# A vision tower on one core: expert shares spread by DMA instead of by matmul, and a new order of work in the last stage

## The chip, the cores and the metric

One core of a Trainium2 chip runs the whole program in one launch. The metric is device time in microseconds (us), median of the runs. TensorE (PE) multiplies matrices, VectorE (DVE), ScalarE (ACT) and GpSimd (POOL) do elementwise work, SyncE (SP) issues most DMAs. Each engine works through its own list of instructions in order; semaphores tie the lists together.

## The reference, cut to what matters

Four images of 3136 patches plus two class tokens go through a token embedding, a state-space layer, an expert layer that picks 1024 tokens per expert, then windowed attention and a second expert layer. The change touches this last part:

```python
# windowed attention: windows of 64 tokens, 8 heads of 16
out = softmax(q k * SCALE) v ;  h = h + (out @ w_proj.T + b_proj)
# second expert layer, on n = layernorm(h)
h_shared = swiglu(n @ shared_in_w.T);  out_shared = h_shared @ shared_out_w.T
# a group of 4 experts per token, softmax over its 4, the best 2 kept, shares normalised
comb[token, expert], cnt[token, expert]            # share, and 0/1 for "chosen"
h_expert = swiglu(n @ expert_in_w.T)
routed = cnt @ expert_out_bias + sum_e comb[:, e] * (h_expert @ expert_out_weight[e].T)
```

All eight experts share `h_expert`, so expert e costs one scaling of `h_expert` by its share (VectorE) and one product with its weights (TensorE), summed in one PSUM bank.

## The kernel before, in words

The program has three stages, one after the other on every engine: phase A (state-space layer), phase B (first expert layer), phase C (`phase_c`, attention and second expert layer). Phase C works on 12,800 token rows as 25 groups of 512 columns (`NG`, `GW`). It is a software pipeline of turns: in one turn `L` is the group whose rows are loaded and normalised, `A` the group in attention, `N` the group whose heads are projected and normalised again, `U` the group whose hidden rows are made (eight products `up0` to `up7`) and whose gates are read, `X` the group that goes through the experts. Four turns fill the pipeline, four drain it. Inside a turn, every engine's list is an order written out by hand at the end of its function; `BANK_ORDER` must tell the same order of use for each of the eight PSUM banks.

What the steps of the prediction touch:

- `turn_o` (L1653) transposes the attention result on TensorE, `keep_o` (L1790) copies it to SBUF as `ot`, SP writes it to DRAM (`heads`, L1586), waits, and reads it back in another order with eight DMAs (`dealt`, L1589). `project` (L1691, L1695) multiplies `dealt` by the projection weights and adds the residual `x` by four products with the identity. SP's list holds, ahead of L1586, the store of the previous group's result (L1567), which waits for `finish` on VectorE (L1900).
- `choose_experts` writes shares, in three copies on partitions 32, 64 and 96 of `cc`, and the 0/1 rows. `turn_choice` (L1638) transposes them. ScalarE and VectorE split the shares into three bf16 parts that add up to the fp32 value (L1777, L1939, L1783, L1944). For each expert `spread` (L1672) multiplies by a selection matrix, so that row e stands on all 128 partitions of a PSUM bank (`CB0`, `CB1`). `scale` (L1957) multiplies the two hidden tiles by it, into a ring of three (`sc`), and `expert` (L1680) multiplies by the expert's weights.
- On ScalarE, after `center` and `variance`: `square`, `norm_rows` (L1834) for group L, `column_scale` (L1841, L1843), `silu_table` (L1797), `affine` (L1848); at the start of the next turn `silu(0)`, `keep_n3` (L1769).
- POOL makes attention's products: scores (L2089) from each `qkv_copy`, and values (L2096) once VectorE's `probs` (L1983) is done.
- Before phase C's first turn SP waits for phase B's last scatter, then issues 13 loads of weights (L1573, L1574), then the first rows (L1579).

An fp32 product appears as two MATMUL records in the trace, a bf16 product and a transpose as one.

Of the kernel before, what the change touches and what calls it, by code (L numbers as in the profile page):

```python
# [17 lines left out]
P = 128  # L18
# [67 lines left out]
def build(nc, a, out, upto="C", debug=None):  # L86

    debug = debug or {}
    with ExitStack() as ctx:
# [893 lines left out]
def phase_b(nc, ctx, mem, a, h_rows, n_rows, logits, after_a, progs):  # L983
# [103 lines left out]
    def sync(sp):  # L1087
# [16 lines left out]
    def vector(dve):  # L1104
# [49 lines left out]
        for r in range(DIGITS):  # L1154
# [218 lines left out]
    def gpsimd(pool):  # L1373
        after_a(pool)
        pool.memset(ones[:], 1.0).then_inc(s_fill, 1)
# [24 lines left out]
        for e in range(E0):  # L1400
            if e + XG - 1 < E0:
# [46 lines left out]
def phase_c(nc, ctx, mem, a, h_rows, out, after_b, progs):  # L1448
# [10 lines left out]
    SC_RING = 3  # L1459
    ident, cen_w, mean_w = sb("ident", [P, P]), sb("cen_w", [P, P]), sb("mean_w", [P, P])  # L1460
    w_qkv = sb("w_qkv", [P, 3 * D])
    w_proj = sb("w_proj", [P, D])
    w_up = sb("w_up", [P, 4 * HF])
    w_so = sb("w_so", [P, 2, D])
    w_ex = sb("w_ex", [P, 2, E1 * D])
    w_gate = sb("w_gate", [P, NGATE])
    gate_b = sb("gate_b", [P, NGATE])
    bias9 = sb("bias9", [E1 + 1, D])
    cols = sb("cols", [P, 3])
    eps_cols = sb("eps_cols", [P, 2])  # L1470
    picks = sb("picks", [P, E1])
# [702 lines left out]
```

## Time and profile before

| | |
|---|---|
| median of 3 runs | 2853.29 us (2849.75 to 2855.03) |
| the profiled execution | 2854.72 us, its span 2852.9 us |
| phase C in it | from the first load at 1819.89 us to the end |
| busy share of the span | PE 85%, DVE 82%, POOL 68%, ACT 54% |
| mean granted TensorE clock | 0.934 of full speed |

Shares over the span average three stages with different limits, so they don't say what bounds phase C; the windows of that phase do. A group's busy time counts overlapping records once.

### The profile page before, as it was taken

The page shows a single profiled execution, that of the slowest core. Times are in us where ns is not written, and L with a number is a line of the kernel's source. Part 1 is how long each engine was busy: PE and PEld are TensorE (multiplying, and loading weights), DVE is VectorE, ACT ScalarE, POOL GpSimd, SP SyncE. Part 2 cuts the span into 40 slices and gives each one's busy share as a digit, 9 for nine tenths or more (in the row PEclk, how much of TensorE's full clock was granted, in tenths as well). Part 3 has the DMA queues.
Part 4 walks back from the last instruction along what each step waited for, and adds up shares of the span by engine and source line. Part 5 has one row for each costly group of instructions (what it writes and reads, how often), then busy time and mean ns, then how long its engine had stood idle before and what let it go on. Part 6 is the DMA issues. An engine that isn't in the chain of part 4 may idle for free. (4 is left out here: it accounts for less than half of the span.)

```text
span 2852.9 us, 25309 instructions
## 1 busy us (share of the span) xinstructions
PE 2417.9 (85%) x6774; PEld 1128.9 (40%) x6774; DVE 2351.7 (82%) x3447; ACT 1544.7 (54%) x2598; POOL 1946.2 (68%) x1008
## 2 busy tenths in 40 slices
PE   5999999999999999999861397159999999899988
PEld 2444444444444444444321143024444444444443
DVE  2999999999999999999978522158887888888875
ACT  4777777777776777777632153134344444344332
POOL 2898898988989889898950388565555555555540
PEclk8999999999999999999975598559999999999999
DMA  2333433334333333433320043300101000011000
GB/s 75 101 120 92 124 105 113 108 95 123 103 112 106 104 118 100 124 98 110 114 82 0 20 70 56 57 22 26 30 30 30 26 28 24 26 30 30 26 23 11
DMA packets 169759, 199.28 MB, mean 70 GB/s; under 512 B 38969, under 2 KB 156946, under 8 KB 169490
## 3 DMA queue, kind: packets, MB, share of 16 engines
q1 hardware_dynamic: 158354, 189.27, 21.6%
q0 software_dynamic: 11264, 8.40, 2.2%
q8 instruction: 56, 0.92, 0.1%
q14 instruction: 85, 0.70, 0.1%
HBM read 164.37 MB, written 33.25 MB: 69 GB/s over the span
## 5 line engine op out<-in xcount | busy, mean ns | idle before, releaser
L915 POOL TENSOR_TENSOR a_hc<-a_h,a_cs 128x896 f32<-128x896 f32 (+1 forms) x448 | 859.5, 1938 | 55.8 <-DVE a_h L778 55.6
L362 PE MATMUL a_y_bank<-a_hc,a_ident 128*128 128x448 f32 (+1 forms) x1792 | 741.8, 544 | 21.8 <-DVE a_yz L798 21.2
L553 ACT ACTIVATE a_da<-a_dt,a_neg_a 128x448 f32<-128x448 f32 (+1 forms) x896 | 551.9, 631 | 296.0 <-DVE a_h L778 291.0
L778 DVE TENSOR_TENSOR_SCAN a_h<-a_da,a_h,a_dbx 128x448 f32<-128x448 f32 x528 | 582.9, 1133 | 9.5 <-ACT a_da L553 4.4
L2096 POOL TENSOR_TENSOR c_prod<-c_prob,c_qkv 128x1024 f32<-128x1024 f32 x100 | 280.8, 2848 | 272.2 <-DVE c_prob L1983 272.2
L362 PEld LDWEIGHTS a_y_bank<-a_hc,a_ident 128*128 128x128 f32 x1792 | 331.5, 190 | 326.3 <-issue 272.6
L1680 PE MATMUL c_p_ACC<-c_sc,c_w_ex 128*128 128x512 f32 x800 | 363.7, 592 | 0.0
L762 DVE TENSOR_TENSOR a_dbx<-a_dtx,a_b_bank 128x896 f32<-128x896 f32 (+1 forms) x308 | 327.3, 1063 | 16.2 <-PE a_b_bank L355 16.1
L2089 POOL TENSOR_TENSOR c_prod<-c_qkv 128x1024 f32<-128x1024 f32 x100 | 231.8, 2341 | 153.2 <-ACT c_qkv L1764 153.2
L1957 DVE TENSOR_TENSOR c_sc<-c_hid,c_p_CB 128x1024 f32<-128x1024 f32 x200 | 240.0, 1214 | 68.5 <-PE c_p_CB L1672 65.8
L903 POOL TENSOR_TENSOR a_dbp<-a_dtx,a_bs 128x896 f32<-128x896 f32 (+1 forms) x140 | 270.9, 1935 | 0.0
L778 DVE TENSOR_TENSOR_SCAN a_h<-a_da,a_h,a_dbp 128x448 f32<-128x448 f32 x240 | 263.1, 1128 | 0.0
L1680 PEld LDWEIGHTS c_p_ACC<-c_sc,c_w_ex 128*128 128x128 f32 x800 | 151.7, 190 | 182.0 <-issue 179.4
L1613 PE MATMUL c_p_W<-c_fl,c_w_up 128*128 128x512 f32 x400 | 211.3, 624 | 9.5 <-ACT c_fl L1848 8.2
L1758 ACT ACTIVATE c_act_half<-c_p_W 128x512 f32<-128x512 f32 x100 | 59.9, 599 | 251.0 <-PE c_p_W L1613 248.9
L405 PE MATMUL a_work<-a_xn,a_w_tap 128*128 128x448 f32 (+1 forms) x448 | 187.3, 552 | 3.7 <-ACT a_xn L694 3.7
L355 PE MATMUL a_b_bank<-a_bc,a_sel 128*128 128x448 bf16 (+1 forms) x308 | 110.2, 358 | 73.5 <-DVE a_dbx L762 71.5
L1385 POOL DMA_INDIRECT b_xg<-n_rows,b_index x64 | 62.3, 974 | 141.2 <-DVE b_tab L1255 122.0
L1991 DVE TENSOR_REDUCE c_o<-c_prod 128x128 f32<-128x1024 f32 x100 | 117.2, 1211 | 38.7 <-POOL c_prod L2096 38.7
L1964 DVE TENSOR_REDUCE c_score<-c_prod 128x64 f32<-128x1024 f32 x100 | 121.2, 1212 | 20.2 <-POOL c_prod L2089 18.0
L932 POOL TENSOR_TENSOR a_spl<-a_spl,a_yt 128x896 f32<-128x896 f32 (+1 forms) x28 | 58.6, 2094 | 90.3 <-DVE a_yt L805 68.0
L1764 ACT COPY c_qkv<-c_p_T 128x384 f32<-128x384 f32 x100 | 49.0, 490 | 130.7 <-PE c_p_T L1645 123.1
(304 smaller groups left out, 3718.2 us busy)
## 6 DMA issues: line engine op xcount, KB each, us to landing
a_cs<-c_rows SPq DMA_DIRECT2D x96, 896.0 KB, 5.2
a_bs<-c_rows SPq DMA_DIRECT2D x24, 1120.0 KB, 5.6
a_cs<-c_rows SPq DMA_DIRECT2D x16, 900.0 KB, 4.4
c_x<-h_rows SPq DMA_DIRECT2D x25, 256.0 KB, 2.7
heads<-c_ot SPq DMA_DIRECT2D x25, 256.0 KB, 2.3
c_dealt<-heads SPq DMA_DIRECT2D x200, 32.0 KB, 1.9
rolled<-c_res SPq DMA_DIRECT2D x25, 256.0 KB, 2.1
h_rows<-a_th SPq DMA_DIRECT2D x24, 224.0 KB
```

Of the source, the lines that this page charges most:

```text
L362: pe.matmul(y_bank[:, d, 0:g.w], ident[:], hc[:, (g.i * NS + n) % HC_RING, d, 0:g.w], start=(n == 0), stop=(n == NS - 1)).then_inc(s_sum, 1)
L405: mm = pe.matmul(tile_of(use, p)[:, 0:w], w_tap[:, j, d * P:(d + 1) * P], xn[:, j:j + w], start=(j == 0), stop=(j == KC - 1))
L553: act.activation(da[:, k % DA_RING, 0:g.w], dt[g.slot][:, d, 0:g.w], ACT.Exp, scale=neg_a[:, d * NS + n:d * NS + n + 1]).then_inc(s_da, 1)
L762: dve.tensor_tensor(dbx[:, k % DBX_RING, :, 0:g.w], dtx[g.slot][:, :, 0:g.w], b_bank[:, 0:g.w].unsqueeze(1).to_broadcast([P, 2, g.w]), ALU ...
L778: dve.tensor_tensor_scan(h[:, n, d, 0:g.w], da[:, (g.i * 2 * NS + k) % DA_RING, 0:g.w], x, state, ALU.mult, ALU.add).then_inc(s_scan, 1)
L903: pool.tensor_tensor(dbp[:, k % DBP_RING, :, 0:g.w], dtx[g.slot][:, :, 0:g.w], bs[:, POOL_STATES.index(n), 0:g.w].unsqueeze(1).to_broadcas ...
L915: pool.tensor_tensor(hc[:, (q.i * NS + n) % HC_RING, :, 0:q.w], h[:, n, :, 0:q.w], cs[:, n % C_RING, 0:q.w].unsqueeze(1).to_broadcast([P, ...
L1613: end(f"up{m}", U, pe.matmul(p[:], w_up[:, m * P:(m + 1) * P], fl[U % 2][:], start=True, stop=True))
L1680: mm = pe.matmul(p[:], w_ex[:, i, e * D:(e + 1) * D], sc[:, k % SC_RING, i, :], start=False, stop=(e == E1 - 1 and i == 1))
L1957: dve.tensor_tensor(sc[:, k % SC_RING, :, :], hid[X % 2][:, 2:4, :], tile_of(f"cb{e}", X)[:].unsqueeze(1).to_broadcast([P, 2, GW]), ALU.mu ...
L2089: pool.tensor_tensor(prod[j][:].rearrange("p (h g d) -> p h g d", h=NH, g=NH), q.rearrange("p (h d) -> p h d", d=DH).unsqueeze(2).to_broad ...
L2096: pool.tensor_tensor(prod[j][:].rearrange("p (h d g) -> p h d g", h=NH, g=NH), prob[:, j * NH:(j + 1) * NH, :].unsqueeze(2).to_broadcast([ ...
```

## The change

- **Shares.** The 0/1 rows now stand three times (partitions 0, 32, 64) and the shares once, on partitions 96 to 103. ScalarE's `keep_choice` copies the shares to `c_s` (fp32) and the 0/1 rows to `c_b` (bf16). SP writes `c_s` to DRAM (`share_out`, 16 KB). ScalarE then waits for that DMA in `share_in` and issues, from its own queue, two DMAs of 1 MB that read four share rows each and write them to all 128 partitions (`c_all`, ring of four halves). The eight `spread` products, the bf16 splitting, `sel_e`, `picks` and the two `CB` banks go.
- **Hidden rows.** The two expert tiles of `hid` are written to the two freed banks (`hx`, in PSUM). `scale(e)` multiplies `hx` by the share row in SBUF.
- **Biases.** One bf16 product of the 0/1 rows with three bf16 parts of the biases, in place of one fp32 product.
- **Projection.** The residual goes first, by four transposes into the projection's bank, and the product with `dealt` is added after its wait. The bank is now `T`, not `M`.
- **Order.** `BANK_ORDER` and all lists of a turn are new. SP stores the previous result after it has issued `heads`. On ScalarE `column_scale` comes ahead of `norm_rows`, and `silu_table` last, behind `affine`.
- **Loads.** Phase C's weights are loaded in phase B (SP's list, at its third expert); their tiles are allocated ahead of phase B's. POOL's first memsets in phase B wait for an early VectorE count.

```diff
-BANK_ORDER = (("up0", "W0", "U"), ("up1", "W1", "U"), ("n3", "T", "A"), ("up2", "W0", "U"), ("up3", "W1", "U"),
...
+BANK_ORDER = (("n3", "T", "A"), ("up0", "W0", "U"), ("qkv0", "M", "A"), ("qkv1", "T", "A"), ("up1", "W1", "U"),
+              ("up2", "W0", "U"), ("trans", "M", "X"), ("gates", "R", "U"), ("o", "M", "N"), ("qkv2", "T", "A"),
+              ("up3", "W1", "U"), ("qkv3", "M", "A"), ("up4", "W0", "U"), ("acc", "ACC", "X"), ("up5", "W1", "U"),
+              ("up6", "W0", "U"), ("proj", "T", "N"), ("cen", "M", "N"), ("up7", "W1", "U"), ("var", "T", "N"))
...
 # SP, one turn
+            load()
+            share_out()
+            heads_out()
+            store_last()
+            heads_in()
...
 # ScalarE
+            def share_in():
+                if X is not None:
+                    act.wait_ge(s_rows[X % 2], (X // 2 + 1) * 16)
+                    for half in range(2):
+                        if X >= 2:
+                            for e in range(half * EG, half * EG + EG):
+                                scaled(act, X - 2, e)
+                        r = X % 2 * 2 + half
+                        act.dma_start(c_all[:, r, :, :], share_rows[X % 2][half * EG:(half + 1) * EG, :].partition_broadcast(P)
+                                     ).then_inc(s_all[r], 16)
...
 # VectorE
+                    dve.tensor_tensor(sc[:, n % SC_RING, :, :], hx[:], shares(dve, X, e), ALU.mult
+                                      ).then_inc(s_sc, 1)
...
 # TensorE
+                    for j in range(GT):
+                        pe.matmul(p[:, j * P:(j + 1) * P], x[N % 3][:, j, :], ident[:], is_transpose=True,
+                                  start=(j == 0), stop=False, skip_group_check=True)
                     pe.wait_ge(s_dealt[N % 2], (N // 2 + 1) * (16 * 8))
+                    mm = pe.matmul(p[:].rearrange("c (w h a) -> c w h a", h=NH, a=8), w_proj[:],
+                                   dealt[N % 2][:].rearrange("p h (w a) -> p w h a", a=8), start=False, stop=True,
+                                   skip_group_check=True)
```

The new lists of a turn, TensorE: `turn_n3, up(0), qkv_mm(0), qkv_mm(1), up(1), up(2), turn_choice, gates, turn_o, qkv_mm(2), up(3), qkv_mm(3), up(4), shared, up(5), up(6), biases, project, expert(0) to expert(5), center, up(7), variance, expert(6), expert(7)`. ScalarE: `keep_n3, silu(0), qkv_copy(0), keep_choice, qkv_copy(1), keep_o, qkv_copy(2), silu(1), share_in, qkv_copy(3), silu(2), silu(3), exp_table, gate_exp, row_scale, score_exp, keep_h3, square, column_scale, norm_rows, affine, silu_table`. VectorE: `choose_experts, sum_values(N, 2), sum_values(N, 3), hidden(0), finish_last, stats_of, sum_scores(0), choose_group, hidden(1), sum_scores(1), sum_scores(2), scale(0) to scale(2), sum_scores(3), scale(3), less_top, scale(4), scale(5), probs, scale(6), scale(7), hidden(2), less_mean, sum_values(A, 0), hidden(3), rescale, sum_values(A, 1)`.

## Rows read from the trace of the kernel before

**Rows 1.** Busy time of each engine in one turn, and in 21 turns.

```profile
core 0: us, PE busy (x) PEld busy (x) DVE busy (x) ACT busy (x) POOL busy (x), PEclk, DMA share, GB/s
2501.78:2538.51 36.73, 34.46 (x105) 16.32 (x104) 31.91 (x68) 15.40 (x29) 20.56 (x9) 1.00 0.10 29
1969.89:2763.84 793.95, 737.54 (x2175) 352.05 (x2174) 668.88 (x1418) 320.05 (x580) 428.31 (x167) 0.98 0.09 28
```

**Rows 2.** Timeline of one turn: start, duration, engine, line.

```profile
2498.13 0.60 PE L1653 MATMUL c_p_M<-c_ident,c_o 128*128 128x128 f32 x4
...
2499.19 1.06 ACT L1790 COPY c_ot<-c_p_M 128x512 f32<-128x512 f32 x1
...
2501.78 0.36 SPq L1567 DMA_DIRECT2D rolled<-c_res  x1
...
2502.18 0.43 SPq L1586 DMA_DIRECT2D heads<-c_ot  x1
...
2504.50 3.63 SPq L1589 DMA_DIRECT2D c_dealt<-heads  x8
...
2509.71 1.10 PE L1691 MATMUL c_p_M<-c_dealt,c_w_proj 128*128 128x512 f32 x2 [2.02 <-DMA c_dealt<-heads]
...
2534.86 0.60 PE L1653 MATMUL c_p_M<-c_ident,c_o 128*128 128x128 f32 x4
```

**Rows 3.** Groups of instructions in the 21 turns.

```profile
L1957 DVE TENSOR_TENSOR c_sc<-c_hid,c_p_CB 128x1024 f32<-128x1024 f32 x168 | 202.1, 1214 | 48.7 <-PE c_p_CB L1672 46.0
...
L1691 PE MATMUL c_p_M<-c_dealt,c_w_proj 128*128 128x512 f32 x42 | 30.0, 806 | 49.1 <-DMA c_dealt<-heads 49.1
...
L1939 DVE TENSOR_TENSOR c_p_M<-c_p_M,c_c_b 40x512 f32<-40x512 f32 x21 | 14.9, 709 | 14.4 <-ACT c_c_t L1778 14.4
```

**Rows 4.** The chain that ended last: start, duration, what.

```profile
2510.80 0.89 PE c_p_M L1695 x8
...
2812.99 1.72 PE c_p_ACC L1680 x4
2814.93 1.72 PE c_p_ACC L1680 x4
```

**Rows 5.** Windows of 2 us behind a wait for `dealt`.

```profile
2052.00:2054.00 2.00, 2.00 (x8) 1.48 (x7) 1.35 (x2) 0.00 (x0) 0.00 (x0) 0.50 0.00 0
```

**Rows 6.** Timeline at the start of phase C.

```profile
1819.89 0.33 SPq L1573 DMA_DIRECT2D c_ident<-in_ident  x1
...
1826.97 1.53 SPq L1579 DMA_DIRECT2D c_x<-h_rows  x3
...
1832.59 0.87 DVE L1912 BATCH_NORM_STATS2 c_stats<-c_x 128x6 f32<-128x128 f32 x4
```

**Rows 7.** DMA issues: KB each, median us from issue to landing.

```profile
a_cs<-c_rows SPq DMA_DIRECT2D x96, 896.0 KB, 5.2
a_bs<-c_rows SPq DMA_DIRECT2D x24, 1120.0 KB, 5.6
...
c_rows<-a_bcr SPq DMA_DIRECT2D x24, 84.0 KB, 5.2
```

**Rows 8.** Timeline of the last turn.

```profile
2828.53 0.19 DVE L2047 TENSOR_TENSOR c_cc<-c_share,c_p_R 128x48 f32<-128x48 f32 x1
...
2833.22 3.48 DVE L1957 TENSOR_TENSOR c_sc<-c_hid,c_p_CB 128x1024 f32<-128x1024 f32 x3 [0.56 <-PE c_p_CB L1672]
```

**Rows 9.** Timeline of ScalarE at the end of a turn.

```profile
2522.99 1.65 ACT L1834 ACTIVATE c_n<-c_x,c_shift,c_rstd 128x128 f32<-128x128 f32 x4 [3.38 <-DVE c_shift L1925]
...
2524.54 0.67 ACT L1841 ACTIVATE c_lv<-c_p_T,c_eps_cols 128x512 f32<-128x512 f32 x1
...
2525.96 1.28 ACT L1797 ACT_TABLE_LOAD   x1
...
2527.26 0.81 ACT L1848 ACTIVATE c_fl<-c_u,c_cols 128x512 f32<-128x512 f32 x1
...
2532.38 0.59 ACT L1769 COPY c_nt<-c_p_T 128x512 f32<-128x512 f32 x1 [0.70 <-PE c_p_T L1620]
```

More of the change, by code:

```diff
@@ L1445, in bank_table @@
     return nth
-def phase_c(nc, ctx, mem, a, h_rows, out, after_b, progs):
+SHARE, PARTS = 96, (0, 32, 64)
+KB = PARTS[-1] + E1 + 1
+@dataclass
+class Fixed:
+    ident: object
+    cen_w: object
+    mean_w: object
+    w_qkv: object
+    w_proj: object
+    w_up: object
+    w_so: object
+    w_ex: object
+    w_gate: object
+    gate_b: object
+    cols: object
+    eps_cols: object
+    earlier: object
+    later: object
+    bias9: object
+    bias_b: object
+    cc: object
+    s_in: object
+    s_const: object
+    loads: int
@@ L1496, in phase_c @@
     act_half = [sb(f"act_half{i}", [P, GW]) for i in range(2)]
-    hid = [sb(f"hid{s}", [P, 4, GW]) for s in range(2)]
-    cc = sb("cc", [P, GT, P])
-    c_t = sb("c_t", [E1 + 1, GW])
+    hid = [sb(f"hid{s}", [P, 2, GW]) for s in range(2)]
     c_b = sb("c_b", [P, GW], BF16)
+    c_s = sb("c_s", [P, GW])
+    c_all = sb("c_all", [P, ALL_RING, EG, GW])
     sc = sb("sc", [P, SC_RING, 2, GW])
@@ L1542, in phase_c @@
     s_sq, s_lv, s_r12, s_fl = map(sem, ("sq", "lv", "r12", "fl"))
-    s_route, s_gexp, s_c_b, s_c_r, s_c_m, s_comb, s_ex = map(
-        sem, ("route", "gexp", "c_b", "c_r", "c_m", "comb", "ex"))
-    LOADS = 13
+    s_route, s_gexp, s_c_s, s_comb, s_ex, s_sc = map(
+        sem, ("route", "gexp", "c_s", "comb", "ex", "sc"))
+    s_rows = [sem(f"rows{s}") for s in range(2)]
+    s_all = [sem(f"all{r}") for r in range(ALL_RING)]
     R_DIF, R_END = 8, 24
@@ new lines, in sync, with load, store, store_last @@
+        for X, U, N, A, L in turns:
+            def load():
+                if L is not None:
+                    if L >= 3:
+                        result(sp, "proj", L - 3)
+                    sp.dma_start(x[L % 3][:], h_rows[L * GW + SHIFT:(L + 1) * GW + SHIFT, :].rearrange(
+                        "(j p) d -> p j d", p=P)).then_inc(s_x[L % 3], 16)
+            def store(c):
+                if c is not None and c >= 0:
+                    taken(sp, "acc", c)
+                    sp.dma_start(out[:, c * GW:(c + 1) * GW], res[c % 2][:]).then_inc(s_res[c % 2], 16)
+            def store_last():
+                if X:
+                    store(X - 1)
+            def heads_out():
+                if N is not None:
+                    taken(sp, "o", N)
+                    sp.dma_start(heads[N % 2], ot[:]).then_inc(s_heads[N % 2], 16)
+            def heads_in():
+                if N is not None:
+                    s = N % 2
+                    sp.wait_ge(s_heads[s], (N // 2 + 1) * 16)
+                    for j in range(8):
+                        sp.dma_start(dealt[s][j * DH:(j + 1) * DH, :, :],
+                                     heads[s][:, j, :].rearrange("(h d) c -> d h c", d=DH)).then_inc(s_dealt[s], 16)
+            def share_out():
+                if X is not None:
+                    sp.wait_ge(s_c_s, X + 1)
+                    sp.dma_start(share_rows[X % 2], c_s[SHARE:SHARE + E1, :]).then_inc(s_rows[X % 2], 16)
+            load()
[3 more added lines that the diff above has]
+            heads_in()
@@ L2065, in vector @@
             scale(2)
-            stats_of()
             sum_scores(3)
```

331 lines of the change are left out of this document (162 added, 169 removed), and 5 rows, old and new, of the table BANK_ORDER.

## The prediction

> **What bounds the kernel now.** I read phase C alone, since phases A and B keep their work. The windows come first [rows 1]: in a turn of 36.73 us TensorE is busy for 34.46, VectorE for 31.91, POOL for 20.56. No engine fills the turn, so something goes round in it. The timeline [rows 2] shows what. Follow one heads trip: `turn_o` ends at 2498.73, the copy `ot` at 2500.25, SP issues `heads` only at 2502.18, it has landed when the eight `dealt` DMAs begin at 2504.50, and `project` starts at 2509.71, after TensorE stood idle for 2.02. That is 10.98 us. From there TensorE works without a gap worth naming to the end of the next `turn_o` at 2535.46, 25.75 us. The two make 36.73: this loop is the turn. The mean of 21 turns is 793.95 / 21 = 37.81 [rows 1], 1.08 more. [...]
>
> So an instruction off TensorE's list counts only if it lies in the 25.75, and time off the heads trip counts in full.
>
> **The first part of the loop, 10.98 us.** In SP's new list the store (L1567) no longer stands ahead of `heads`. From the end of `ot` to the issue passed 2.18 less 0.25, 1.93 us, while SP waited for `finish` and issued the store [rows 2]; only some 0.05 of it stays, but I leave that out. `share_out` now stands ahead of `heads`; its data are ready before `turn_o` starts, and its issue of 0.4 us (as L1567) is over by then. So 9.05 us.
>
> New here is traffic. `share_in` issues 2 MB some 2.4 us behind `turn_o`, just as `heads` is on its way and before `dealt` is issued. The nearest rows [rows 7]: 896 KB land in 5.2 us and 1120 KB in 5.6, so I take 5.4 for the first megabyte, and the second about 3 us later. All eight `dealt` DMAs then share the engines with it. How much later `dealt` lands no row shows. Lower bound 0. Upper bound: `dealt` is served behind both megabytes, which land at about 2.4 + 0.4 + 8.4 = 11.2 us after `turn_o`, plus a little, against 9.05: 2.5 us. The nearest row for a small DMA in such company is `c_rows`, 84 KB in 5.2 us [rows 7], where `heads` with 256 KB and no company takes 2.32 [rows 2]; but it is behind big ones in the same queue. [...]
>
> [...]
>
> **The second part, 25.75 us.**
> - Six of the eight spreads lie in it. One costs what it adds between two experts: 2814.93 - 2812.99 - 1.72 = 0.22 [rows 4]. 6 x 0.22 = 1.32 off. (VectorE's idle waits for a spread, 48.7 us in 21 turns [rows 3], lie beside TensorE's work and give nothing more.)
> - The residual's eight records, 0.89 [rows 4], go ahead of the wait, where TensorE idles: 0.89 off.
> - `up(6)` moves ahead of the wait and `up(3)` behind `turn_o`. Two products (four records) take 1.72 [rows 4], one 0.86: 1.72 off.
> - `qkv_mm(1)` (384 columns of 512: 0.65), `turn_choice` (four transposes, about 0.44) and `gates` (eight small records, 0.89 as the residual's eight) move into it: 1.98 on.
> - `turn_o` now follows `turn_choice` in bank M and must wait for both copies of `keep_choice`, 0.6 us each (as L1769 [rows 9]) and hand-overs, 1.3 against `gates` 0.89: 0.4 on.
> - A new wait: `qkv_mm(0)` now comes second, after `up(0)`, and needs `keep_n3`. On ScalarE it stands behind a row of work that starts when `variance` ends: hand-over 0.2, the two passes of `column_scale` 1.4 (2524.54 to 2525.96), `norm_rows` 1.65, `affine` 0.81, the table 1.28, `keep_n3` 0.59 [rows 9], together 5.9. Before, the table load stood in the wait for `affine`'s input and cost nothing; `affine` now waits behind `norm_rows`, so that cover is gone. TensorE meanwhile has experts 6 and 7 (3.44), four transposes 0.44, `up(0)` 0.86: 4.75. Queued behind it: `qkv_copy(0)`, and POOL's score products. 1.15 on.
>
> Sum: 25.75 - 1.32 - 0.89 - 1.72 + 1.98 + 0.4 + 1.15 = 25.35. Adding up forward what the new list holds from `project` to `turn_o` gives 24.8 (no small friction in it; the same for the old list gives 25.2 against 25.75). I take 25.05, and keep 24.8 and 25.35 as ends.
>
> **The loop.** 9.05 + 25.05 = 34.1. With 0.6 for traffic 34.7, and 1.1 for clock and stray long turns as before (the idle wait ahead of `project` is much the same: 9.65 less the 7.1 us of work behind `turn_o` and a stall or two) 35.8. Against 37.81: 2.0 a turn.
>
> **Other loops that could be longer.** VectorE: 31.91 less two splitting passes of 0.71 [rows 3] is 30.5. `scale` keeps one operand in PSUM and one in SBUF, so I leave 1.21 us; were it 10% dearer, 1 us a turn, still under 34.1. TensorE: 34.46 less 8 x 0.22 less 0.4 for the residual less 0.9 for the biases, 31.4. POOL: the value products start when `probs` is done, `qkv_copy(0)` waits for them, then come the score products, together 20.56 [rows 1], then on VectorE a reduction of 1.2 and what leads to `probs`; with copies about 26 us. All under 34.1. The old first wait in VectorE's turn, for POOL, is covered by `choose_experts`, which now comes first.
>
> **The shares' trip.** `turn_choice` ends; `c_s` 0.6; DMA to DRAM about 2.2 (nearest: 2.32 for `heads` [rows 2]); ScalarE reaches `share_in` 4.2 us after `turn_choice` because of the copies ahead of it, so the landed rows aren't waited for; then 5.4. `scale(0)` can start 9.6 us after `turn_choice`, `expert(0)` at 10.9. `project` begins 0.9 + 0.4 + 0.44 + 9.05 = 10.8 after it and ends 0.86 later. So 0.8 us is spare: hidden, barely. Uncovered, each further us costs one per turn.
>
> **The ends.** Start: 13 loads stood ahead of the rows; L1579 moves from 1826.97 to 1819.89 and `stats_of` no longer waits for the last weight. With the 2.32 that 256 KB of `heads` take [rows 2] it starts at 1822.3 against 1832.59 [rows 6]: 10 off. If the load took the 5.2 of `c_rows` [rows 7], it would be 7. The loads in phase B run beside a stage whose wait is not for SP; POOL's wait there is for an early VectorE count, long before its lists are used: 0. Filling: the turn of X = 0 gains a full turn's 2. Drain: in the last turn nothing covers the shares' trip. Shares to `scale(0)` took 4.5 us [rows 8]; now 0.8 + 0.6 + 2.2 + 5.4 = 9, and `expert(0)` waits for the first scaling too: 4.3 later, with 1.8 of spreads back. With the turn before: 2 on.
>
> **Sum.** 22 x 2.0 = 44, 10, 2, less 2: 54 off the profiled execution's 2854.72, 2801; the median of the runs is 1.4 lower, so **2799 us**.
>
> **The rivals.**
> - **The wait for `dealt` shrinks and the clock stays up.** The traffic costs nothing, the idle wait is 1 us, the clock never falls: 33.85 to 34.1 a turn, 3.8 x 22 = 84 and 10: 2759, down to 2750. For it: the store was 1.93 of the trip. Against: 2 MB a turn. 0.25.
> - **The traffic eats the gain.** `dealt` lands behind the megabytes: 2.5 on, and the longer idle lets the clock fall every turn, 1.6 on (a half-clock stretch of some 3 us, of which [rows 5] shows two, costs half its length): 38.2, or 37.4 if it falls in half of them. 22 x 0.4 either way, and 10: 2834 to 2852, its middle 2843. [...] 0.18.
> - **The shares come late (slower).** Place: `scale(0)` behind `c_all`. If a megabyte from ScalarE's queue takes over 10 us in place of 5.4, the 0.8 spare is gone, the turn is over 38.3 with the clock's share, and the start's 10 us are used up. At 11 us: 22 x 1.2 less 10: 2870. Against: 1120 KB landed in 5.6 [rows 7]. 0.09.
> - **Nothing moves** (the loop is another than I think, all edits beside it): only the start, 2843. 0.03.
>
> The forecast has 0.45, its own range 2780 to 2818 (traffic 0.2 to 1.4, second part 24.8 to 25.35). The whole range, 2755 to 2845, leaves out the late shares, half of the first rival's lower end and part of the second's upper. A measurement of this kernel tells 0.2% (6 us) from no change. Faster: 0.45 + 0.25 + most of 0.21 = 0.86; same 0.05; slower 0.09.
>
> **What would show it.** Heads trip near 9.6 us, `heads` issued within 0.1 of `ot`; `project`'s idle wait of 1.5 to 2.5; a gap of about 1 us before `qkv_mm(0)` put down to `keep_n3`; `dealt` landing later behind its last issue than before; `c_all` at 5 to 6; `stats_of` at 1823; DVE busy near 30.5 a turn. It is wrong if `scale` waits for `c_all` in each turn, if `dealt` lands 2 us later, or if VectorE rather than the heads trip closes the turn.

## The result, and the profile after

The changed kernel takes 2907.18 us (median of 4 runs, 2905.07 to 2910.9), against 2852.88 beside it: a ratio of 1.0185, interval 1.0167 to 1.0203. It is slower by 54 us, where the forecast was faster by 54.

The windows, with the columns of [rows 1]: one turn, then 20 turns.

```profile
2566.79:2607.70 40.91, 33.67 (x93) 15.68 (x92) 32.67 (x67) 14.94 (x28) 20.52 (x9) 0.92 0.24 78
1993.04:2811.64 818.60, 667.28 (x1810) 310.81 (x1809) 649.78 (x1307) 295.47 (x531) 405.99 (x159) 0.92 0.23 77
```

A turn is 818.60 / 20 = 40.93 us, against 37.81 before and 35.8 in the forecast. TensorE is busy for less time than before [rows 1], though at half clock for part of it, and waits more. The timeline of one turn, as [rows 2], shows where:

```profile
2564.00 0.28 SPq L1688 DMA_DIRECT2D share_rows<-c_c_s  x1
...
2565.33 1.06 ACT L1885 COPY c_ot<-c_p_M 128x512 f32<-128x512 f32 x1 [0.37 <-PE c_p_M L1756]
...
2566.14 0.33 ACTq L1877 DMA_DIRECT2D c_c_all<-share_rows  x1
2566.41 0.34 SPq L1675 DMA_DIRECT2D heads<-c_ot  x1
...
2566.63 0.71 ACTq L1877 DMA_DIRECT2D c_c_all<-share_rows  x1
2566.79 0.56 SPq L1666 DMA_DIRECT2D rolled<-c_res  x1
...
2572.22 3.48 DVE L2034 TENSOR_TENSOR c_sc<-c_hx,c_c_all 128x1024 f32<-128x1024 f32 x3
...
2573.18 4.02 SPq L1682 DMA_DIRECT2D c_dealt<-heads  x8
...
2578.63 2.08 PE L1790 MATMUL c_p_T<-c_dealt,c_w_proj 128*128 128x512 f32 x2 [5.89 <-DMA c_dealt<-heads]
...
2600.58 0.88 PE L1748 MATMUL c_p_M<-c_w_qkv,c_nt 128*128 128x384 f32 x2 [0.86 <-ACT c_nt L1857]
```

`heads` is issued 0.02 us behind the copy `ot`: the store is out of its way, as forecast. But `dealt` begins only 6.77 us later, where 2.32 had passed before [rows 2]. `project` starts 13.34 us behind `turn_o` (its end, 2565.29, is 0.04 ahead of the copy), where 9.05 was expected without traffic. The first megabyte was issued 0.27 us *ahead* of `heads`. ScalarE's DMA issue doesn't stand behind its copy in progress: L1877 is issued at 2566.14, 0.25 us before the copy ends at 2566.39, and `silu(1)`, ahead of it in the list, only starts at 2566.59.

The page's list of DMA issues (KB each, median us to landing), as [rows 7], shows that every transfer that starts there is slow; `dealt`, issued when the megabytes are nearly through, isn't:

```profile
c_c_all<-share_rows ACTq DMA_DIRECT2D x50, 1024.0 KB, 7.5
...
heads<-c_ot SPq DMA_DIRECT2D x25, 256.0 KB, 7.3
c_dealt<-heads SPq DMA_DIRECT2D x200, 32.0 KB, 1.9
rolled<-c_res SPq DMA_DIRECT2D x25, 256.0 KB, 8.5
```

Windows of 2 us behind `heads` (the last three columns are granted clock, DMA share, GB/s):

```profile
2567.00:2569.00 2.00, 2.00 (x6) 0.87 (x5) 1.76 (x9) 1.26 (x3) 2.00 (x2) 1.00 0.98 213
2569.00:2571.00 2.00, 2.00 (x5) 0.68 (x4) 1.93 (x4) 0.01 (x1) 2.00 (x2) 1.00 0.96 354
2571.00:2573.00 2.00, 1.74 (x8) 0.79 (x6) 2.00 (x3) 0.86 (x2) 0.98 (x1) 1.00 1.07 440
2573.00:2575.00 2.00, 0.00 (x0) 0.00 (x0) 2.00 (x3) 1.59 (x4) 0.00 (x0) 1.00 0.83 322
2575.00:2577.00 2.00, 0.00 (x0) 0.00 (x0) 1.82 (x2) 0.00 (x0) 0.00 (x0) 0.77 0.31 69
2577.00:2579.00 2.00, 0.37 (x1) 0.37 (x2) 0.00 (x0) 0.00 (x0) 0.00 (x0) 0.50 0.20 44
2579.00:2581.00 2.00, 2.00 (x3) 0.80 (x3) 0.00 (x0) 0.00 (x0) 0.00 (x0) 0.50 0.00 0
```

The DMA engines are full for some 6 us. Then TensorE idles for 5.89 us, its granted clock falls from 1.00 to 0.50, and the first work behind the wait runs at that. The groups over the 20 turns, as [rows 3]:

```profile
L1790 PE MATMUL c_p_T<-c_dealt,c_w_proj 128*128 128x512 f32 x40 | 41.5, 1141 | 122.8 <-DMA c_dealt<-heads 122.8
...
L1748 PE MATMUL c_p_M<-c_w_qkv,c_nt 128*128 128x384 f32 x78 | 33.0, 504 | 16.4 <-ACT c_nt L1857 16.4
```

The wait is 122.8 / 20 = 6.1 us a turn (before 49.1 / 21 = 2.3), and `project`'s mean of 1141 ns, against 806 [rows 3] and 646 in b_store_later, whose turns are all at full clock, says that it is at half clock in nearly every turn.

### The profile page after: what moved, and what is told of

Read it like the earlier page. It is cut to its first block, busy times and chain, and to the rows that moved or that the text cites. A ratio compares the mean times of both kernels' runs of the same rounds, so it can differ in the third digit from the quotient of the medians.

```text
span 2905.2 us, 24738 instructions
## 1 busy us (share of the span) xinstructions
PE 2366.6 (81%) x6449; PEld 1097.3 (38%) x6449; DVE 2361.2 (81%) x3406; ACT 1533.1 (53%) x2573; POOL 1944.5 (67%) x1008
## 4 chain that ended last, share of the span: by engine, by line
PE 19%; DMA 8%; ACT 6%; POOL 5%; DVE 5%; issue 4%; SPq 3%; another core or an unknown queue 0%; DVEq 0%; ACTq 0%; POOLq 0%
PE c_p_ACC L1776 10%; DMA heads<-c_ot 6%; POOL h_rows L1400 3%; SPq L1682 3%; PE c_p_W L1716 2%; PE c_p_T L1790 2%; DMA c_dealt<-heads 2%; ACT c_n L1930 1%; POOL b_xg L1390 1%; DVE b_seen L1133 1%; ACT L1892 1%; PE c_p_T L1805 1%; ACT c_ot L1885 1%; PE c_p_M L1748 1%; PE c_p_M L1799 1%
## 5 line engine op out<-in xcount | busy, mean ns | idle before, releaser
L2034 DVE TENSOR_TENSOR c_sc<-c_hx,c_c_all 128x1024 f32<-128x1024 f32 x200 | 237.7, 1219 | 194.4 <-PE c_p_ACC L1776 176.3
L1776 PE MATMUL c_p_ACC<-c_sc,c_w_ex 128*128 128x512 f32 x800 | 381.9, 634 | 9.2 <-DVE c_sc L2034 9.2
L1776 PEld LDWEIGHTS c_p_ACC<-c_sc,c_w_ex 128*128 128x128 f32 x800 | 167.0, 209 | 232.3 <-issue 220.4
L1716 PE MATMUL c_p_W<-c_fl,c_w_up 128*128 128x512 f32 x400 | 205.2, 616 | 1.8 <-ACT c_act_half L1846 0.6
L1790 PE MATMUL c_p_T<-c_dealt,c_w_proj 128*128 128x512 f32 x50 | 50.9, 1121 | 147.9 <-DMA c_dealt<-heads 147.9
L1909 ACT ACTIVATE c_expo<-c_score 128x256 f32<-128x256 f32 x25 | 10.4, 417 | 255.8 <-DVE c_score L2049 255.8
L1400 POOL DMA_INDIRECT h_rows<-b_og,b_index x64 | 100.8, 1575 | 27.0 <-issue 18.3
```

What stands on the lines that cost most here:

```text
L1400: pool.indirect_dma_start(h_rows[:, :], bass.IndirectOffsetOnAxis(ap=index[:, i, e:e + 1], axis=0), og[e % 2][:, i, :], None, compute_op=A ...
L1716: end(f"up{m}", U, pe.matmul(p[:], w_up[:, m * P:(m + 1) * P], fl[U % 2][:], start=True, stop=True))
L1776: mm = pe.matmul(p[:], w_ex[:, i, e * D:(e + 1) * D], rows[:, i, :], start=False, stop=(e == E1 - 1 and i == 1))
L2034: dve.tensor_tensor(sc[:, n % SC_RING, :, :], hx[:], shares(dve, X, e), ALU.mult).then_inc(s_sc, 1)
```

## The experiments

Each ratio is to the kernel before, run beside it, with its 95% interval.

### How much the transfers cost

**a_small.** From the third group on each of the two shares' DMAs brings 64 KB.

```diff
+                        n, w = (EG, GW) if X < 2 else (1, P)
-                        act.dma_start(c_all[:, r, :, :], share_rows[X % 2][half * EG:(half + 1) * EG, :]...
+                        act.dma_start(c_all[:, r, 0:n, 0:w], share_rows[X % 2][half * EG:half * EG + n, 0:w]...
```

> The changed kernel with the shares' two DMAs cut from 1 MB to 64 KB each from the third group on (the experts then use old shares; the output is not the reference's). Every wait and every list stays. Theory traffic: heads lands 6.7 us after its issue in the changed kernel, against 2.3 before, because the 2 MB share its 16 DMA engines; without them it lands in 2.3 again, the turn is 40.9 - 4.4 = 36.5 and, as the idle wait of TensorE ahead of the projection shrinks from 5.9 to 1.5 us, the clock falls less: 35 to 36.5 a turn, 2780 to 2810 us in all. Rival order: the new lists and bank order make the turn long; then heads or its successor still closes it at 39 to 41 a turn, 2860 to 2907. Rival store: the store now issued 0.4 us behind heads in the same queue slows it: heads then stays over 4 us.

Measured 2821.3 us, 0.991 (0.9892 to 0.9927): above the 2780 to 2810 expected, for `heads` landed after 4.2 us and not after 2.3. The bytes taken out are worth 86 us, and something still stood in the trip: the small DMAs or the store.

**a_no_dma.** The two DMAs are left out from the third group on, and with them the scalings' wait for new shares (the experts use old ones, as in a_small).

```diff
-                    for half in range(2):
+                    for half in range(2 if X < 2 else 0):
...
-        eng.wait_ge(s_all[r], (c // 2 + 1) * 16)
+        eng.wait_ge(s_all[r], 16)
```

> The changed kernel with the shares' two DMAs left out altogether from the third group on (old shares are used; the output is not the reference's); with 64 KB each heads still took 4.3 us at the median. Theory traffic: even those two small DMAs, which read the same DRAM row 128 times, held heads up by 2 us; without any, heads lands in 2.1 to 2.4, the turn is 2 us and more shorter than there, 34 to 35.5 in place of 37.1: 2760 to 2785 us. Rival: the store issued 0.4 us behind heads holds it up; then heads still takes 4 us and the time is 2815 to 2825.

Measured 2745.81 us, 0.9622 (0.9597 to 0.9648), below the 2760 to 2785 expected. The wait for `dealt` is 1.0 us a turn, `project`'s mean 645 ns. So the new lists without the traffic win 107 us, and the two megabytes take 161 back. The store is still issued 0.4 us behind `heads` here, and `heads` lands after 2.0 us: it wasn't the store that made 4.2 of it in a_small, but two DMAs of 64 KB.

### Is it the traffic, and where

**b_decoy, b_decoy_plain, b_decoy_late.** The kernel *before*, with two DMAs of 1 MB from ScalarE's queue whose data nobody reads: repeated rows, issued some 1.5 us ahead of `heads`; as many bytes from addresses that don't repeat; and the repeated rows again, issued behind `square`, some 20 us ahead of the next `heads`.

```diff
+            def decoy():
+                if X is not None:
+                    for r in range(2):
+                        need(act, s_all[r], 16 * X)
+                        act.dma_start(c_all[:, r, :, :], <1 MB of weights>).then_inc(s_all[r], 16)
             silu(2)
+            decoy()
             keep_choice()
```

> The kernel before, and beside its work two DMAs of 1 MB a turn from ScalarE's queue, DRAM rows repeated over 128 partitions into a tile that nobody reads, issued about 1 us ahead of heads. Everything else is the kernel before. Theory traffic: heads lands 3 to 5 us later, the turn of 37.8 gets 3 to 6 us longer with the clock's share, 2920 to 2980 us. If the new lists and not the traffic made the changed kernel slow, this one stays within 1% of before, 2853 to 2880.

> The kernel before plus two DMAs of 1 MB a turn at the same place as in the decoy with repeated rows, but from 1 MB of distinct DRAM addresses to the same tile. If bytes on the 16 engines are what delays heads, this costs the same as repeated rows: 2990 to 3020 us, heads at 6 to 8 us. If it is the 128-fold reading of one place, heads comes sooner, the kernel is below 2960.

> The kernel before with the decoy of 2 MB a turn issued behind square, some 20 us ahead of heads, in place of just ahead of it. Theory traffic by place: nothing on the loop meets it, heads lands in 2.3 as before, within 0.5% of before (2845 to 2865 us), against +5.4% at the other place. If bytes cost as such (ports of SBUF, DRAM), it stays slow, over 2900.

Measured 3005.07 us (1.0543, 1.0526 to 1.0561), 3004.41 (1.0521, 1.0491 to 1.0551) and 2850.05 (0.9996, 0.998 to 1.0011). `heads` landed after 8.0, 7.9 and 2.3 us. The first is dearer than the 2920 to 2980 expected. So it is the bytes, not the repeated reading, and the place is all: the same 2 MB cost 152 to 157 us or nothing.

**b_store_later, b_store_x.** The kernel before, with two parts of the change alone: SP issues `heads` ahead of the store; and then also the residual by transposes ahead of the wait.

```diff
-            if X:
-                store(X - 1)
             if N is not None:
                 ...
                 sp.dma_start(heads[s], ot[:]).then_inc(s_heads[s], 16)
+            if X:
+                store(X - 1)
```

> The kernel before with one edit: SP issues heads first and the previous group's store behind it. The 1.93 us between the end of ot's copy and the issue of heads go; the turn is closed by the heads trip, so 1.5 to 1.9 a turn, with TensorE's idle wait near 0.3 the clock seldom falls: 37.8 to 35 to 36 a turn, 2790 to 2820 us. Rival: another wait (VectorE, POOL) is right behind and takes the place: over 2835.

> As b_store_later, and the residual by four transposes ahead of the wait for dealt, as the change has it. It takes 0.9 from TensorE's list behind the wait, and the work ahead of it gets 0.44 longer: where the idle wait was 2.0 and is now near 0.2, TensorE is the bound and the gain is only what its list gets shorter, 0.4 to 0.9 a turn: 10 to 20 us below b_store_later.

Measured 2803.7 us (0.9817, 0.979 to 0.9844) and 2800.27 (0.9814, 0.9788 to 0.9841). The store's place alone is worth 49 us. The group of `project` in 21 turns of b_store_later, then the windows of 20 turns, of b_store_later and of b_store_x (last three columns as above):

```profile
L1692 PE MATMUL c_p_M<-c_dealt,c_w_proj 128*128 128x512 f32 x42 | 23.7, 646 | 2.2 <-DMA c_dealt<-heads 2.0
...
1972.50:2684.59 712.09, 690.13 (x2081) 324.90 (x2080) 636.26 (x1361) 307.55 (x561) 410.96 (x161) 1.00 0.10 30
...
1965.64:2677.90 712.26, 680.55 (x2001) 316.72 (x2000) 636.29 (x1361) 307.53 (x561) 411.00 (x161) 1.00 0.10 30
```

A turn is 712.09 / 20 = 35.60 us at full clock, against the 36.73 of the full-clock turn and the mean of 37.81 before. So the clock gave its 1.08 back whole, but of the trip's 1.93 us only 1.13 came: 2.21 together, times 22 is 49. What stopped it is a second loop that the heads trip isn't in. Pieces of the chain of waits before, behind the `project` of [rows 2]:

```profile
2520.08 7.73 POOL c_prod L2096 x3
...
2528.49 2.87 POOL c_prod L2096
...
2537.88 0.61 DVE c_res L1900
```

From the first scaling the chain goes through VectorE to `probs`, through POOL's value products, back to VectorE and to `finish` (L1900), for which the store ahead of `heads` waited. With the store out of the way the chain of b_store_later runs through VectorE's scalings, `probs` and POOL's products from turn to turn, without `heads`, `dealt` or `project`. That is also why the residual ahead of the wait wins some 3 us, within what can be told, and not 10 to 20: b_store_x turns in 712.26 / 20 = 35.61 us, although TensorE has 9.6 us less to do in the 20 turns.

### Which DMA of the trip pays

**a_after_heads.** ScalarE waits until `heads` has landed before it issues the megabytes (and stands behind `qkv_copy(3)`).

```diff
+                    if N is not None:
+                        act.wait_ge(s_heads[N % 2], (N // 2 + 1) * 16)
```

> The changed kernel with one wait more: ScalarE issues the shares' DMAs only when heads has landed in DRAM (share_in stands behind qkv_copy(3)). All 2 MB still flow, now beside the eight small dealt DMAs. If it is the one write of 256 KB that suffers from company, heads lands in 2.3, the turn gets up to 4 us shorter (37 to 38.5 a turn), 2820 to 2850 us. If any small DMA suffers as much, dealt lands 3 to 5 us late instead and nothing is won: 2890 to 2910. Shares come 2.3 us later than now, which costs up to 1 us a turn if the projection comes at 9.5 us behind the transposed attention rows.

Measured 2907.49 us, 1.0207 (1.0189 to 1.0224). `heads` 2.1 us, but `dealt` 6.6: nothing won, as its second expectation had it.

**a_heads_on_act.** `heads` issued from ScalarE's queue, just ahead of the megabytes there.

```diff
             keep_o()
+            heads_out()        # act.dma_start(heads[N % 2], ot[:])
             qkv_copy(2)
```

> The changed kernel with heads issued by ScalarE's queue, right behind its copy and ahead of the shares' DMAs, so that it stands first in the same rings. Theory traffic: in its own queue nothing is ahead of it, it lands in 2.3 to 3.5 us, and only dealt runs beside the megabytes: 37 to 38.5 a turn, 2820 to 2850 us. If the engines' bandwidth, and not the queue's turn, is what delays it, heads lands in 4 to 6 us still and the kernel stays above 2870.

Measured 2859.01 us, 1.0037 (1.0025 to 1.0048). `heads` 2.1, `dealt` 5.4: better by 48, but short of the 2820 to 2850 expected.

**shares_early.** The choice and the shares' trip are moved a turn's part earlier: `choose_experts` behind `probs`, `turn_choice` between experts 6 and 7, `share_in` at the end of ScalarE's turn. `keep_choice` goes to VectorE, and `turn_o` ahead of `up(2)` and `gates`.

```diff
             probs()
+            choose_experts()   # for U, no longer for X at the turn's start
             scale(6)
...
             silu_table()
+            share_in()         # ScalarE, end of the turn
```

> The changed kernel with the shares' trip moved to the previous turn: VectorE chooses a group's experts behind probs, TensorE transposes them between experts 6 and 7, VectorE copies them to SBUF, and the 2 MB flow some 6 us ahead of the next heads. turn_o comes ahead of up(2) and gates. Theory traffic: the megabytes are free where no small DMA on the loop runs beside them; heads lands in 2.0 to 2.5, and with the shorter list ahead of turn_o the turn is 33 to 35: 2720 to 2770 us. If 2 MB a turn cost as such, wherever they flow, heads or the weights' users get slower again and the kernel stays above 2800.

Measured 2850.82 us, 1.0002 (0.9985 to 1.002): a miss. The wait for `dealt` was down to 20.4 us in 20 turns, though `heads` still took 3.4 us (median): in the turn below the megabytes are issued at 2567.33, 5 us ahead of it. But another loop closed. Pieces of that kernel's chain of waits (start, duration, what):

```profile
2549.14 1.22 DVE c_sc L2023
...
2551.66 0.20 DVE c_p_R L2088
...
2555.62 2.28 DVE c_sc L2023 x2
2558.02 0.71 DVE c_hx L2012
2558.77 2.08 PE c_p_W L1717 x2
2560.85 1.34 PE c_p_T L1805 x2
...
2567.33 0.33 ACTq L1867
2567.70 0.59 ACT c_nt L1857
```

The 4 us of the choice (2551.66 to 2555.6) now stand on VectorE ahead of the last scalings and `hidden(2)`; `up(7)` waits for its bank, `variance` stands behind it, then ScalarE's work and `keep_n3`.

### Order of issue or bytes

**a_half_late, a_act_half_late.** The second megabyte (experts 4 to 7) is issued by SP behind the eight `dealt` DMAs. The first stays on ScalarE's queue. The second kernel also has `heads` on ScalarE's queue, as a_heads_on_act.

```diff
 # ScalarE, share_in
-                    for half in range(2): ...
+                    act.dma_start(c_all[:, X % 2 * 2, :, :], share_rows[X % 2][0:EG, :].partition_broadcast(P)...
 # SP
             heads_in()
+            sp.dma_start(c_all[:, X % 2 * 2 + 1, :, :], share_rows[X % 2][EG:2 * EG, :].partition_broadcast(P)...
```

> The kernel after, but the second megabyte of shares (experts 4 to 7) is issued from SyncE's queue behind the eight dealt DMAs; the first stays on ScalarE's queue. The same bytes, one half of them outside the heads trip. Theory (what costs is the bytes in flight beside heads and dealt): heads lands after 4.5 to 5.5 us in place of 7.3, the wait ahead of project falls from 5.9 to about 3, the turn from 40.9 to 38.5, about 2850 us. Rival (any large broadcast, wherever it lies, costs about the same): 2895 to 2910. Rival (the second half lands too late for the fifth scaling): VectorE waits for c_all there, 2870 or more.

> As a_heads_on_act (heads issued from ScalarE's queue ahead of the shares), with the second megabyte of shares issued from SyncE's queue behind the eight dealt DMAs. Theory: heads stays at 2.1 us, the first megabyte is through after some 4 to 5 us, so dealt's own landing falls from 5.4 to 2 to 3 and the wait ahead of project from 3.6 to 1 to 1.5; with less half clock some 2.5 us a turn: 2800 to 2815 us, as fast as the best version of the kernel before. Rival (the second megabyte collides with the result's store and the next rows, or comes late for the fifth scaling): 2850 or more.

Measured 2907.1 us (1.02, 1.0178 to 1.0222) and 2771.93 (0.9727, 0.9705 to 0.975). The first is a miss that taught most: half of the bytes are out of the trip, and nothing is won. `heads` still took 6.4 us. A turn of a_half_late in the timeline:

```profile
2557.61 0.33 ACTq L1887 DMA_DIRECT2D c_c_all<-share_rows  x1
...
2557.89 0.33 SPq L1675 DMA_DIRECT2D heads<-c_ot  x1
...
2566.59 3.48 DVE L2044 TENSOR_TENSOR c_sc<-c_hx,c_c_all 128x1024 f32<-128x1024 f32 x3 [2.83 <-DMA c_c_all<-share_rows]
2566.70 3.63 SPq L1682 DMA_DIRECT2D c_dealt<-heads  x8
```

`scale(0)`, which waits for the megabyte, and `dealt`, which waits for `heads`, start 0.11 us apart. The 256 KB, issued 0.28 us behind the megabyte on another queue, land with it (after 8.8 us in this turn; the medians are 6.2 us for the megabyte and 6.4 for `heads`).

The DMA packets by queue tell more (packets, MB, share of the 16 engines; q10 is ScalarE's, q1 is SP's). From the issue of `heads` at 2517.02 to 2521.50, then to 2523.50, about when it lands:

```profile
q10 hardware_dynamic: 106, 0.87, 84.5%
q1 hardware_dynamic: 1, 0.00, 0.1%
...
q1 hardware_dynamic: 282, 0.52, 67.0%
q10 hardware_dynamic: 38, 0.18, 21.7%
```

For 4.5 us the engines carry the megabyte, and one packet of SP's queue; then `heads` and the store come through in 2 us, as fast as in a_no_dma (0.52 MB from 2502.5 to 2504.5). Over 17 turns the first packet of `heads` starts 4.3 us (median) behind its issue, in 21 turns of a_no_dma 0.84. So `heads` doesn't share the engines with the megabyte, and it isn't only its end that is late: it starts when the megabyte ahead is nearly through. Three kernels take this apart.

**a_half_behind.** As a_half_late, with one wait more, so that the megabyte comes 0.8 us behind `heads`.

```diff
                     act.wait_ge(s_rows[X % 2], (X // 2 + 1) * 16)
+                    if U is not None:
+                        taken(act, "up2", U)      # waits for ScalarE's copy silu(1)
```

> As a_half_late (heads on SyncE's queue, first megabyte on ScalarE's, second behind the dealt DMAs), but ScalarE waits for its copy silu(1) before it issues the first megabyte, so that this is issued some 0.8 us behind heads and not 0.3 us ahead. Queues and bytes as in a_half_late. Theory (who is issued first decides): heads lands after 2 to 3 us, dealt after 2.6 to 3.5, 2765 to 2800 us. Rival (heads and the store of the result share SyncE's queue and lose to ScalarE's): heads stays above 5 us, 2880 to 2910.

**a_half_store_later.** As a_half_late, with the store last.

```diff
             heads_out()
-            store_last()
             heads_in()
             share_in_late()
+            store_last()
```

> As a_half_late, with the store of the previous result moved behind the dealt DMAs and the second megabyte, so that only one megabyte is beside heads. Theory (the megabyte ahead decides): heads still 5 to 6.5 us, 2880 to 2907. Rival (the store's 256 KB in the same queue was what held heads): heads 2 to 4 us, below 2850.

**a_act_half_first.** As a_act_half_late, with `share_in` ahead of `heads_out` in ScalarE's list.

```diff
             keep_o()
+            share_in()
             heads_out()
             qkv_copy(2)
             silu(1)
-            share_in()
```

> As a_act_half_late, with the first megabyte ahead of heads in ScalarE's queue, not behind it; every DMA keeps its queue. Theory (order decides): heads waits for the megabyte and lands after 6 to 8 us, 2890 to 2920 us, against 2772 in the other order. Rival (what made a_act_half_late fast is that only one megabyte is beside the trip, or the queue of heads): within 20 us of 2772.

Measured 2769.66 us (0.9712, 0.9695 to 0.9729), 2880.56 (1.01, 1.0081 to 1.0118) and 2870.51 (1.007, 1.0048 to 1.0093). The same queues, the same bytes, and 1.1 us of order are worth 137 us (2907.1 to 2769.66). The store's 256 KB, issued 0.4 us *behind* `heads`, are worth 27: what follows that closely still costs some. Inside one queue the order is worth 99 (2771.93 to 2870.51).

**a_behind.** The kernel after with that one wait more: both megabytes, behind `heads`. **a_half_behind_store.** As a_half_behind, with the store last as well.

> The kernel after with one wait more: ScalarE waits for its copy silu(1) before share_in, so that both megabytes are issued some 0.8 us behind heads in place of just ahead. Nothing else differs. By order: heads lands after 2.1 us in place of 7.3, but dealt, issued into the midst of two megabytes, lands after 5 to 5.5 (5.4 in a_heads_on_act): 2850 to 2865 us. So order is worth some 50 us, and the half moved behind dealt the other 90. If order alone is all, 2775 or less.

> As a_half_behind, with the result's store behind the second megabyte (as in a_half_store_later). The 256 KB of the store leave the trip: dealt 2.6 to 3.0 in place of 3.2, 2755 to 2768 us. Rival: the store now runs beside the next rows and the second megabyte and nothing is won, 2770 us.

Measured 2877.74 us (1.0083, 1.0059 to 1.0106) and **2759.59 us (0.9671, 0.9649 to 0.9693)**, the fastest of all, faster than both kernels. a_behind is 13 us above its forecast: `dealt` took 6.0 us, not 5 to 5.5. With both megabytes in the trip the order alone is worth 29 us (2907.18 to 2877.74), not the 50 expected; moving the second one behind `dealt` is worth another 108. Neither does it alone: a_half_late, with the move and without the order, won nothing. The kernels with the new lists, side by side (medians of landings; the wait is the group of `project`, over 19 to 21 turns):

| kernel | ahead of `heads` | behind `heads`, ahead of the last `dealt` | `heads` us | `dealt` us | wait a turn, us | time, us |
|---|---|---|---|---|---|---|
| after | 1 MB, and 1 MB 0.2 us behind | store | 7.3 | 1.9 | 6.1 | 2907 |
| a_half_late | 1 MB | store | 6.4 | 1.8 | 5.7 | 2907 |
| a_half_store_later | 1 MB | - | 5.7 | 1.8 | 4.9 | 2881 |
| a_act_half_first | store, 1 MB | - | 5.3 | 1.8 | 3.8 | 2871 |
| a_after_heads | - | store, 2 MB beside the first `dealt` | 2.1 | 6.6 | 6.1 | 2907 |
| a_behind | - | 2 MB, store | 2.0 | 6.0 | 4.7 | 2878 |
| a_heads_on_act | store (1.1 us) | 2 MB | 2.1 | 5.4 | 3.7 | 2859 |
| a_act_half_late | store (1.1 us) | 1 MB | 2.1 | 2.6 | 1.6 | 2772 |
| a_half_behind | - | 1 MB, store | 2.1 | 3.2 | 1.8 | 2770 |
| a_half_behind_store | - | 1 MB | 2.0 | 2.7 | 1.5 | 2760 |
| a_small | 64 KB, and 64 KB 0.2 us behind | store | 4.2 | 1.9 | 2.8 | 2821 |
| a_no_dma | - | store | 2.0 | 1.8 | 1.0 | 2746 |

A turn of a_half_behind_store in the timeline, then its windows (one turn, 20 turns):

```profile
2563.29 0.32 SPq L1675 DMA_DIRECT2D heads<-c_ot  x1
...
2564.14 0.33 ACTq L1889 DMA_DIRECT2D c_c_all<-share_rows  x1
...
2565.29 4.24 SPq L1682 DMA_DIRECT2D c_dealt<-heads  x8
...
2569.16 3.49 DVE L2046 TENSOR_TENSOR c_sc<-c_hx,c_c_all 128x1024 f32<-128x1024 f32 x3
2569.70 0.34 SPq L1697 DMA_DIRECT2D c_c_all<-share_rows  x1
...
2570.98 1.13 PE L1801 MATMUL c_p_T<-c_dealt,c_w_proj 128*128 128x512 f32 x2 [1.33 <-DMA c_dealt<-heads]
```

```profile
2528.88:2563.29 34.41, 31.55 (x92) 14.87 (x91) 32.70 (x69) 14.94 (x28) 20.53 (x9) 1.00 0.30 93
1978.22:2665.87 687.65, 629.30 (x1811) 296.15 (x1810) 650.36 (x1309) 295.73 (x532) 406.52 (x159) 1.00 0.29 92
```

The megabyte lands while SP is still issuing the eight `dealt` DMAs, one every 0.53 us (4.24 us for the eight), and so costs almost nothing. The turn is 687.65 / 20 = 34.38 us at full clock: the 34.1 that the prediction had without traffic, nearly. a_no_dma turns in 33.84 (642.91 us in 19 turns), so the megabytes still cost 0.54 a turn, as much as the wait for `dealt` is longer (1.5 against 1.0). `scale` waits for shares only 3.5 us in these 20 turns, and 20 more in the last turns, where nothing covers their trip. a_no_dma saves those 20, but its first two groups still bring 2 MB each ahead of `heads` and put it 16 us behind by its third turn; in all it is 14 us faster.

## Why the prediction was wrong, point by point

- **"Two make the turn" (heads trip and second part): right for the new lists, incomplete for the old ones.** After the change the chain of waits goes round through just these two, in every version of it but shares_early. Before it, `heads` waited for `finish`, and so for a loop through VectorE and POOL that takes 35.6 us a turn by itself (b_store_later). The prediction adds such a loop up to about 26 us for the new lists, and never for the old ones. With the new lists it doesn't close above the 33.84 of a_no_dma, which is measured; why it is so much shorter there no run takes apart.
- **The store off SP's list, 1.93 a turn:** the issue right behind `ot` came as forecast. Alone, in the old lists, it is worth 49 us, 1.13 a turn and the clock's 1.08, for the other loop closes there.
It comes 2.13 to 2.14 us behind the issue of `share_rows` in 20 turns, so the shares' landing in DRAM is what it waits for. (2) Its victim: the term was put on `dealt`, with `heads` left at 2.32. `heads` paid. `dealt` does land later when it is issued beside the megabytes: after 6.0 us in a_behind in place of 1.9 (in the turn from 2549.60 there, between 2555.46 and 2558.50, ScalarE's queue has 57.7% of the 16 engines' time and SP's 42.6%). The step's upper bound of 2.5 came from one small DMA served behind both megabytes, which land by 11.2 us. Their own landings were taken about right: 5.4 us and about 3 us later, against 5.6 for the first in the turn shown after and 3.4 us later for the second (issued at 2566.63, 8.5 us). But `dealt` can only be issued after `heads` has landed, so the megabytes' time stands ahead of the 4 us of issue and 1.9 of landing, not beside them: 7.3 - 2.3 = 5 on, not 2.5. (3) The size: the 0.6 in the forecast's sum was the author's guess, and no run shows it. Measured: 13.34 us from `turn_o` to `project`, in place of 9.65, and 8.29 in a_no_dma without the traffic: a term of 5.05. A term so small needs `heads` to get through beside the megabyte of the other queue, and a_half_late shows one packet of SP's queue in 4.5 us of ScalarE's megabyte.
- **The first part without traffic, 9.05:** 8.29 in a turn of a_no_dma (2500.78 to 2509.07), better than added up: the copy `ot` now starts 0.02 us behind `turn_o`, where it was 0.46 in [rows 2], and `heads` takes 2.06 in place of 2.32.
- **The second part, 25.05, and the clock.** In the turn shown after, it is 2606.20 - 2578.63 = 27.57 us, in a turn of a_no_dma at full clock 2534.53 - 2509.07 = 25.46, just above the upper end of 25.35. The difference of 2.11 us lies in two rows of the chains of waits, first after, then a_no_dma; behind them both run alike:

```profile
2578.63 2.08 PE c_p_T L1790 x2
2580.70 11.46 PE c_p_ACC L1776 x24
...
2509.07 1.12 PE c_p_T L1790 x2
2510.20 10.30 PE c_p_ACC L1776 x24
```

- The clock was taken at 1.1 a turn as before: the mean turn of before is 1.08 us longer than the one at full clock, the granted clock is 0.50 behind some of its waits [rows 5], and b_store_later, whose 20 turns are all at 1.00, has none of this. With nearly 6 us of idle the clock fell in nearly every turn after (`project`'s mean 1141 ns). The wait for `keep_n3` was foreseen at 1.15 and is 0.86.
- Together 8.29 + 5.05 + 25.46 + 2.11 = 40.91, the turn measured. Against the terms of the forecast's 35.8 (9.05, 0.6, 25.05, 1.1): 4.45 too little for the traffic, 1.0 for the clock, 0.4 for the second part, 0.8 too much for the first. 5.1 x 22 = 113 us: with 54 of forecast gain that is a loss of 59; measured 54.
- **VectorE** shows 32.5 busy, where 30.5 was expected. The difference isn't work: the row of `c_shift`, 4 columns, has a mean of 2710 ns in the 20 turns, where 171 ns stood before, and 2.5 us of it a turn are most likely a wait inside the instruction: in the turn shown it runs from 2592.46 to 2595.18, and one of POOL's value products from 2592.35 to 2595.15; two other turns look the same. No run tests it, and it bounds nothing: a_half_behind_store has the same row (2715 ns) and turns in 34.38.
- **The shares aren't late: right.** VectorE waited 18.1 us for them in the whole phase after.
- **The start: right in size.** `stats_of` begins at 1820.05 in place of 1832.59 [rows 6]; 2.9 us of this are earlier stages that ended sooner in that execution, 9.7 the new loads (forecast 10). In the drain the shares take from 2876.86 to 2884.59, 7.7 us, to `scale(0)` (forecast 9, before 4.5 by [rows 8]).
- **The rivals.** "The traffic eats the gain" had the mechanism, with the wrong DMA and little over half the price: 4.1 us a turn for traffic and clock, where 7.2 came. "The wait shrinks and the clock stays up", 2759, is about what the kernel does once the order is right, half the bytes are behind `dealt` and the store is last. That this one measured 2759.59 is luck in the last digits: its turn is 34.38, not 33.85 to 34.1, and its wait 1.5, not 1. "The shares come late" and "nothing moves" are out.

The choice of queue gains nothing that can be told: a_half_behind and a_act_half_late, with `heads` on SP's queue and on ScalarE's, differ by 2 us (2769.66 and 2771.93). Nor do the packets of two queues run mixed wherever work of both is queued: behind a megabyte that is under way they don't (a_half_late, the packets above), and the same bytes cost 137 us more when they are issued 0.3 us ahead of `heads` and not 0.8 us behind. With the second megabyte, issued 0.2 us behind `heads`, they do: from 2570.00 to 2573.16 in the turn shown after, both queues have packets, 0.95 MB of ScalarE's in 73.1% of the 16 engines' time and 0.32 MB of SP's in 26.0%. In a_half_late the packets of `heads` themselves start late, 4.3 us behind its issue in place of 0.84, and that is enough to explain its landing. What holds them back no run here takes apart.

## What to carry to other kernels

Of a latency-bound DMA (a round trip that TensorE waits for), ask what was issued in the microseconds ahead of it, on any queue: here it landed about when that had landed. Issue the small one first, put a megabyte behind it and into the time in which its successor is being issued, and move the rest past the trip. Both are needed: one wait moved a_half_late by 137 us, but the kernel after, with both megabytes in the trip, by 29. Cost a wait that grows by what it delays in series, and add the clock: 2.1 us a turn behind an idle of 5.89 here. And before you call a loop the turn, ask which loop comes next: taking 1.93 us off this one gave 1.13.

## What the runs showed of the hardware that was not expected

- 256 KB issued 0.28 us behind a megabyte on another queue land after 6.4 us (median), 0.8 us ahead of it after 2.1, in place of 2.0 alone. In the first case one packet of their queue moves in 4.5 us, while the megabyte takes 84.5% of the DMA engines' time. Two DMAs of only 64 KB, one just ahead of it and one 0.2 us behind, already make 4.2 of it (a_small). There the packets of both queues run mixed, those of `heads` from 1.1 us behind its issue on, and the engines are busy for only 42% of the time from 2513.50 to 2516.27; why so much for so little stayed open.
- ScalarE issues a DMA while its own copy is still running: in 20 turns of the kernel after 0.24 to 0.26 us before the copy `ot` ends, and in the turn shown 0.45 us ahead of `silu(1)`, which stands before it in the list.
- The wait for `dealt` costs more than itself. Between a_half_behind and a_heads_on_act it grows by 1.9 us a turn and the kernel by 89 / 22 = 4.1. The rest is mostly time at a lower granted clock: for the same lists TensorE is busy for 472.05 / 14 = 33.7 us a turn in place of 635.59 / 20 = 31.8, at a mean granted clock of 0.93 in place of 0.99, and `project`'s mean goes from 667 to 1097 ns.
- Two megabytes each turn are free in one place of a 38 us turn (b_decoy_late, 2850.05 us) and cost 7 us a turn in another (b_decoy, 3005.07 us).
